# Attention scores as sixteen 32x32 products in four PSUM banks, where four 128x128 products on block-diagonal queries stood

## The reference

```python
qm = _split_heads(q @ Wq.T + bq)      # q = layernorm(x); 16 heads of 32
km = _split_heads(k @ Wk.T + bk)      # k = context, 257 rows
vm = _split_heads(v @ Wv.T + bv)
scores = jnp.einsum('bnlh,bnph->bnlp', qm, km) / np.sqrt(HEAD_DIM)
scores = jnp.where(mask, scores, MASK_FILL)
attn = jax.nn.softmax(scores, axis=-1)
out = jnp.einsum('bnlp,bnph->bnlh', attn, vm)
```

## Time and profile before

| | |
|---|---|
| runs | 1419.02, 1418.9, 1415.56 us, median 1418.9 |
| profiled execution | 1421.52 us, span 1419.4 us |
| busy in the span | PE 1324.6 us (93%), PEld 1020.0 (72%), DVE 774.0 (55%), ACT 632.2 (45%), POOL 392.0 (28%) |
| TensorE instructions | 7110 matmuls, 7111 weight loads |
| granted TensorE clock | 0.981 of full on average |

### The profile page before, as it was taken

The page is one execution under the profiler, slowest core; times in us unless marked ns, Lnnn a source line. Parts: engine busy times, 40 slices in busy tenths (PEclk is TensorE's granted clock), DMA queues, the critical chain, the costliest instruction groups (busy, mean ns, idle before and its releaser), DMA issues. The chain is left out here.

```text
span 1419.4 us, 27453 instructions
## 1 busy us (share of the span) xinstructions
PE 1324.6 (93%) x7110; PEld 1020.0 (72%) x7111; DVE 774.0 (55%) x1808; ACT 632.2 (45%) x1320; POOL 392.0 (28%) x314
## 2 busy tenths in 40 slices
PE   5999999999999999999997888999999999999991
PEld 4888878888888878788886544676677676677670
DVE  4445565565655655655655354665655566655540
ACT  3443344353343433443532114466666566656650
POOL 0001020030030210200300303455555555756441
PEclk9999999999999999999999988999999999999996
DMA  5721110201111101101002105799999999999985
GB/s 199 281 98 32 31 48 17 62 16 39 38 32 31 46 16 31 47 16 54 24 1 71 56 23 208 220 324 324 339 297 303 267 339 306 358 289 314 265 219 87
DMA packets 67184, 204.71 MB, mean 144 GB/s; under 512 B 16047, under 2 KB 18351, under 8 KB 56768
## 3 DMA queue, kind: packets, MB, share of 16 engines
q1 hardware_dynamic: 43248, 159.71, 31.3%
q0 software_dynamic: 23888, 44.40, 14.9%
HBM read 177.26 MB, written 37.03 MB: 151 GB/s over the span
## 5 line engine op out<-in xcount | busy, mean ns | idle before, releaser
L370 POOL TENSOR_TENSOR rstd<-vep,half 128x1 f32<-128x1 f32 x32 | 17.8, 555 | 600.4 <-DVE vep L537 600.3
L856 PE MATMUL bank<-ch,wkh 128*128 128x256 f32 x512 | 160.6, 314 | 8.1 <-DVE cl L548 8.0
L458 ACT ACTIVATE kt<-bank,colb 128x256 f32<-128x256 f32 x128 | 60.5, 472 | 239.1 <-PE bank L858 238.8
L1494 PE MATMUL ebank<-guh,xth 128*128 128x512 f32 x380 | 154.7, 407 | 1.6 <-DVE xtl L1387 1.0
L1382 DVE TENSOR_TENSOR gul<-wgu,guh 128x2048 fp32r<-128x2048 f32 x54 | 123.8, 2293 | 55.3 <-ACT guh L1299 48.4
L1496 PE MATMUL ebank<-guh,xtl 128*128 128x512 f32 x380 | 149.0, 392 | 0.0
L1495 PE MATMUL ebank<-gul,xth 128*128 128x512 f32 x380 | 148.3, 390 | 0.0
L1229 POOL DMA_INDIRECT xg<-xn_rows,ig x95 | 121.3, 1277 | 85.1 <-issue 71.2
L858 PE MATMUL bank<-ch,wkl 128*128 128x256 f32 x512 | 144.3, 282 | 0.0
L857 PE MATMUL bank<-cl,wkh 128*128 128x256 f32 x512 | 144.2, 282 | 0.0
L1524 PE MATMUL ebank<-wd,ht 128*128 128x512 f32 x292 | 134.4, 593 | 0.8 <-ACT ht L1284 0.8
(11 more groups left out here) (247 smaller groups left out, 2817.2 us busy)
## 6 DMA issues: line engine op xcount, KB each, us to landing
wgu<-in_egu SPq DMA_DIRECT2D x54, 1024.0 KB
wd<-in_edn SPq DMA_DIRECT2D x54, 512.0 KB
sgu<-in_egu SPq DMA_DIRECT2D x17, 1024.0 KB
craw<-in_ctx SPq DMA_DIRECT2D x32, 514.0 KB, 3.2
sdn<-in_edn SPq DMA_DIRECT2D x17, 512.0 KB
wqkv<-in_wqkv SPq DMA_DIRECT2D x1, 3072.0 KB, 18.4
second_sums<-x1b SPq DMA_DIRECT2D x9, 256.0 KB, 3.7
xa<-in_x SPq DMA_DIRECT2D x8, 256.0 KB, 2.7
```

Source lines behind the costliest of these rows:

```text
L856: mm(out, wkh[:, c, w], h[:, c, :], start=c == 0, stop=False)
L1494: mm(out, ah[:, c, :], bh[:, c, :], start=c == 0, stop=False)
```

## The change

The scores of a batch become 16 products of a 32x32 weight (the queries of a head, read where the projection left them in `qt`) with 32x257 keys. Product (i, g) uses rows 32i to 32i+31 of the array and its columns 32g to 32g+31, and writes partitions 32g to 32g+31 of bank `sc_ps[i]`. Four banks are used; two of them have other users: bank 0 is also that of the keys and values, and AV moves from bank 5 into the bank of the transposes, bank 4. All 16 stand in slot k = 5, after T1, which is moved there too; AV follows them. `qb`, its zeroing and ACT's four copies a batch go away. As `qt` is now read directly by all four batches, the query projection of the next tile moves from s = 20 of one pass to s = 1 of the next.

```diff
-PRE = {4: "norm", 18: "xT", 20: "q"}
+PRE = {4: "norm", 18: "xT"}
+PREQ = 1
-        kv_ps, sc_ps, at_ps, av_ps, px = bank[0:2], bank[2:4], bank[4], bank[5], bank[6:8]
+        kv_ps, sc_ps, at_ps, av_ps, px = bank[0:2], (bank[2], bank[3], bank[5], bank[0]), bank[4], bank[4], bank[6:8]
...
+                    if front and prev and s == PREQ:
+                        on_pre("q", t)
...
-            def q_blocks(t, b):
-                n = BT * t + b
-                wait(act, s_pqe, t + 1)
-                wait(act, s_sc, 4 * n - 4)
-                for i in range(HG):
-                    r = slice(i * HD, (i + 1) * HD)
-                    last = nc.scalar.copy(qb[b % 2][r, :, i * HD:(i + 1) * HD], qt[r, :, b * L:(b + 1) * L])
-                last.then_inc(s_qb, 1)
...
+                if k == 5 and front:
+                    wait(dve, s_tr, 2 * (n - 1))
+                    wait(dve, s_sc, n + 1)
+                    for i in (HG - 1, *range(HG - 1)):
+                        V.tensor_tensor(prob[b % 2][:, i, :], sc_ps[i][:, 0:S], cap[b % 2][:, :], ALU.min).then_inc(s_sa, 1)
                 if k == 5 and carried:
                     attended(t, b)
-                if k >= 4 and front:
-                    for g in (2 * (k - 4), 2 * (k - 4) + 1):
-
-                        wait(dve, s_sc, 4 * n + g + 1)
-                        if g == 0:
-                            wait(dve, s_tr, 2 * (n - 1))
-                        V.tensor_tensor(prob[b % 2][:, g, :], sc_ps[g % 2][:, 0:S], cap[b % 2][:, :], ALU.min).then_inc(s_sa, 1)
...
+                    if k == 0:
+                        wait(pe, s_sa, 4 * n - 3)
...
+                if k == 5 and carried and front:
+                    prob_t(n, b, 1)
+                if k == 5 and front:
+                    wait(pe, s_ke, 4 * n + 4)
+                    wait(pe, s_ve, 2 * n + 1)
+                    wait(pe, s_sa, 4 * n)
+                    wait(pe, s_pqe, t + 1)
+                    wait(pe, s_pte, t + 2 if b == 3 and nxt else t + 1)
+                    pe.sem_inc(tick, 1)
+                    for g in range(DC):
+                        for i in range(HG):
+                            r = slice(i * HD, (i + 1) * HD)
+                            last = mm(sc_ps[i][g * L:(g + 1) * L, 0:S], qt[r, g, b * L:(b + 1) * L], kt[r, g, :], start=True, stop=True)
+                    last.then_inc(s_sc, 1)
...
-                if k >= 4 and front:
-                    if k == 4:
-                        wait(pe, s_qb, n + 1)
-                    for g in (2 * (k - 4), 2 * (k - 4) + 1):
-                        wait(pe, s_ke, 4 * n + g + 1)
-                        wait(pe, s_sa, 4 * n + g - 1)
...
-                        mm(sc_ps[g % 2][:, 0:S], qb[b % 2][:, g, :], kt[:, g, :], start=True, stop=True).then_inc(s_sc, 1)
-                if k == 4 and carried and front:
-                    prob_t(n, b, 1)
```

More of the change, by code:

```diff
@@ L133, in stage_a @@
         vlc = sb("vlc", [P, DC, NB])
-        qb = [sb(f"qb{i}", [P, DC, P]) for i in range(2)]
+        rows = [sb(f"rows{i}", [P, D]) for i in range(2)]
         prob = d.prob
@@ L163, in stage_a @@
         idx, entry = d.idx, d.entry
-        flat = [a[:, :, :].rearrange("p c s -> p (c s)") for a in (craw[0], craw[1], qb[0], qt, qb[1], xat)]
+        flat = [a[:, :, :].rearrange("p c s -> p (c s)") for a in (craw[0], craw[1], qt, xat)]
+        flat = flat[0:2] + [rows[0][:, :], flat[2], rows[1][:, :], flat[3]]
         sx, sy = [a[:, 0:D] for a in flat[:4]], [a[:, D:2 * D] for a in flat[:2]] + flat[4:]
@@ L168, in stage_a @@
         sht = [wq[:, 3, j * I:(j + 1) * I].rearrange("p (c n) -> p c n", c=IC) for j in range(2)]
-        sd_ps = [at_ps, av_ps]
+        sd_ps = [bank[4], bank[5]]
         s_sl = [sem(f"shared_rows_in{j}") for j in range(SHA)]
@@ L185, in stage_a @@
         s_kv, s_ke, s_ve = sem("kv_projected"), sem("keys_copied"), sem("values_copied")
-        s_qb, s_sc, s_sa = sem("q_blocks"), sem("scores_done"), sem("scores_copied")
+        s_sc, s_sa = sem("scores_done"), sem("scores_copied")
         s_nb, s_ex, s_pn = sem("max_done"), sem("exp_done"), sem("prob_scaled")
@@ L288, in on_pre @@
             def on_pre(n, t):
-                if n == "q":
+                if n == "xT":
                     wait(sp, s_pt, t + 1, tick)
@@ L339, in _ @@
                 load_shared(j, sx[j], sy[j], s_sl[j])
-            sp.wait_ge(s_sc, 4 * NB)
+            sp.wait_ge(s_sc, NB)
             sp.wait_ge(s_pq, NT)
@@ L362, in _ @@
             nc.gpsimd.memset(pad[:, :, 1], 0.0).then_inc(s_pad, 1)
-            for i in range(2):
-                nc.gpsimd.memset(qb[i][:, :, :], 0.0).then_inc(s_pad, 1)
-            pool.wait_ge(s_pad, 4)
+            pool.wait_ge(s_pad, 2)
             def root(n):
@@ L441, in _ @@
             high(0, 0)
-            act.wait_ge(s_pad, 4)
             def exps(b, n, gs):
@@ L456, in per_batch @@
                     wait(act, s_kv, 6 * n + k + 1)
-                    wait(act, s_sc, 4 * n)
+                    wait(act, s_sc, n)
                     nc.scalar.activation(kt[:, k, 0:S1], kv_ps[k % 2][:, 0:S1], ACT.Identity, bias=colb[:, 1, k:k + 1]).then_inc(s_ke, 1)
@@ L461, in per_batch @@
                 if k == 3 and front:
[L462 to L465, removed]
                     if b < 3 or nxt:
@@ L470, in per_batch, with attention @@
                 if k == 4 and carried:
-                    for j in range(2):
-                        wait(act, s_tr, 2 * (n - 1) + j + 1)
-                        nc.scalar.copy(att[:, j, :], at_ps[:, :]).then_inc(s_at, 1)
+                    attention(n, 0)
+                    if not front:
+                        attention(n, 1)
+                if k == 5 and carried and front:
+                    attention(n, 1)
                 if k == 5 and front:
                     values(n, b, k)
-                if k == 5 and front and b == 3 and nxt:
-                    q_blocks(t + 1, 0)
+            def attention(n, j):
+                wait(act, s_tr, 2 * (n - 1) + j + 1)
+                nc.scalar.copy(att[:, j, :], at_ps[:, :]).then_inc(s_at, 1)
             def values(n, b, k):
@@ L655, in on_pre @@
                 if n == "q":
-                    wait(dve, s_qb, 4 * t)
                     pre_q(t)
@@ L877, in per_batch @@
                     wait(pe, s_pn, n)
+                    wait(pe, s_od, n - 1)
                     prob_t(n, b, 0)
@@ L883, in per_batch @@
                     wait(pe, s_ve, 2 * n)
-                    wait(pe, s_od, n - 1)
                     pb = (b - 1) % 2
@@ L887, in per_batch @@
                         w = slice(g * P, (g + 1) * P)
-                        mm(av_ps[:, w], vb[pb][:, 0, w], att[:, 0, w], start=True, stop=False)
-                        last = mm(av_ps[:, w], vb[pb][:, 1, w], att[:, 1, w], start=False, stop=True)
+                        for j in range(2):
+                            heads = att[:, j, :].rearrange("p (i g n) -> p g i n", i=HG, g=DC)[:, g]
+                            last = mm(av_ps[:, w], vb[pb][:, j, w], heads, start=j == 0, stop=j == 1)
                     last.then_inc(s_av, 1)
-                if k >= 4 and front:
-                    if k == 4:
-                        wait(pe, s_qb, n + 1)
-                    for g in (2 * (k - 4), 2 * (k - 4) + 1):
-                        wait(pe, s_ke, 4 * n + g + 1)
-                        wait(pe, s_sa, 4 * n + g - 1)
[L897 to L900, removed]
-                        mm(sc_ps[g % 2][:, 0:S], qb[b % 2][:, g, :], kt[:, g, :], start=True, stop=True).then_inc(s_sc, 1)
-                if k == 4 and carried and front:
-                    prob_t(n, b, 1)
                 if k == 5 and b == 0 and type(t) is int and t == 0:
@@ L912, in on_pre @@
                 if n == "q":
+                    wait(pe, s_sa, 4 * BT * t)
                     pre_q(t)
```

## The result

The changed kernel takes 1489.7 us (median of 4 runs, 1488.97 to 1497.11), the kernel before 1417.7 beside it: a ratio of 1.052, 95% interval 1.049 to 1.055. My 1509 us was in the right direction and inside its range, but that is luck: the 72 us did not come from where I had put them. The sixteen products are far cheaper than the four were, and nearly all of the loss lies in stage B, which the change does not touch.

The account below looks back on a forecast made before the run. PE's list order was taken to bound stage A (busy 739.57 of 762 us). Terms +73 + 27 - 7 - 4 + 1 = +90 us on the median of 1418.9 gave 1509 us, range 1408 to 1522.

Parts of the forecast that it names:

- Only two neighbours overlap: Stage A scores: one product per 0.218 us; with drains 4.03 us a batch against 1.74, +73 us; chance 0.45.
- third rival: Stage A scores: all squares overlap, rows and columns; 1426 us, or 1405 down to 1397 us; chance 0.26.
- The two drains: Array runs empty going from whole-array to small-square matmuls and back, twice a batch: 0.33 us, within the +73 us.
- The change lies wholly in stage A; stage B comes after it and I leave it as it is: Scope of the forecast: only stage A, 14 to 776 us, was given terms; stage B got none.
- The query projection: Moved out of its old place, it leaves T0 waiting for DVE's scaling: 4.5 us in passes 1 to 6, +27 us.
- echo: After T0's wait PE runs some 3 us at 1.2 GHz; T0 to x3T takes 1.38 us more.
- Oproj: Its wait for `ot` falls from 1.3 us to 0.3 or less, 7 times: -7 us.
- T1: Its wait for ACT's copy, 0.14 us in most batches, is covered by half of the values: -4 us.
- oT: Transposes at s = 18 hang on DVE work that now has all four mins ahead of it: +1 us.
- Costed at nothing: ACT's four copies (1.20 us a batch), the first key projection's wait for bank 0, and the later maximum and `nbias`: zero.
- The wait for bank 0: First key projection waits for DVE's reading of scores, covered by AV; without that cover 0.4 us a batch, 13 us.

Follow-up runs that it names:

- the kernel with one row of squares: Changed kernel with 80 extra semaphore increments, all sixteen products reading partitions 0 to 31, so four squares instead of sixteen; measured 1620.5 us.
- the query projection back: Changed kernel with the query projection back at s = 20, a second tile for its result and 74 extra semaphore increments; measured 1410.8 us, ratio 0.995.
- 64 increments: Changed kernel with 64 extra semaphore increments ahead of ACT's loops; measured 1415.5 us, again with ten runs 1418.1 us, ratio 1.0007 to the kernel before.
- 80 increments: Changed kernel with 80 extra semaphore increments at the start of ACT's list; measured 1441.4 us, ratio 1.016 to the kernel before.
- 128 or 208: Changed kernel with 128 or 208 extra semaphore increments ahead of ACT's loops; measured 1499.3 us and 1418.2 us, one run each.
- 58 against 74: Changed kernel with the query projection back at s = 20 and 58 or 74 extra semaphore increments; measured 1403.6 us and 1410.8 us.

## Why the prediction came out as it did

The number was near (1509 for 1489.7, forecast +90, measured +72 beside the same kernel), and for the wrong reason. Two steps failed, by about 104 us one way and 72 the other; that they nearly cancel is luck.

- **"Only two neighbours overlap"**, +73 us, is the step that failed first. From my premise (the second record of a product can't start before the first is through: true, 0.24 us) I went on to "if PE starts its matmuls in the order of the list", and that is not what it does: the next fifteen products' first records start ahead of the second of the first. Starts were to be 0.11 us apart and are 0.0067. The burst takes 0.745 us up to AV. Together with the longer handover from T1 (0.20 for 0.11 us) a batch costs 0.84 us for 1.74. Over stage A the time from start to start falls from 60.1 to 23.8 us for the scores, and rises by 2.9 for the handovers from T1 and by 2.5 for AV: -31 us. That is my third rival, which had 0.26. The Trainium skill's rule in "TensorE: Matmul & The Clock Gate", Part 3, that matmuls stay in program order, was what I leaned on; the starts above do not agree with it for the two records of one fp32 product. Its packing of sixteen squares agrees in kind: it gives the span as one matmul and about 4 ns for each further tile, and here the second record starts 0.24 us behind the first, is 0.375 us long, and the further squares add 15 x 6.7 ns, which makes 0.72 us to the end of the last record.
- **The two drains**, 0.33 us a batch, were about right in size. On the way in, T1's last record holds PE 0.20 us for 0.11. On the way back the changed kernel can't show it: AV starts 0.40 us after the last score record does, but then it is ACT's copy that it waits for. In the kernel with one row of squares, where that copy is long done, AV starts 0.305 us after the last score record, in batches at the full clock, where scores follow each other at 0.217. Its first record then holds PE 0.21 us for 0.11, in both kernels. That is 0.09, 0.09 and 0.10 us, 0.28 in all.
- **"The change lies wholly in stage A; stage B comes after it and I leave it as it is"** failed by 72 us, the whole of the result. The page had the place to ask from: queue 14 fetches instructions, and the change plainly takes instructions out of ACT's list ahead of stage B. Nothing in the profile of before says that a shift of 80 would do harm. It could have been told as a rival with an unknown price; by experiment a bad place costs 72 us in one kernel and 77 in the other.
- **The query projection**, +27 us by 4.5 us a pass. The wait is right: 3.1 us in each of passes 1 to 6. Its echo was under-sized. From the earlier trace rows I took 1.38 us, the part of T0 to x3T alone. In passes 1 to 6 the half clock lasts until the values are well under way, so the starts sum to 26.4 us more for the values, 2.7 for x3T and 5.7 for the router: 35 us, 5.8 a pass. With the query projection back the wait is gone.
- **Oproj**, -7: 5.4 us less wait; the row holds only 6.9 us in six waits, so seven times one was too much. **T1**, -4: the wait for ACT went from 2.0 to 0.7 us, and what handover shrank with it was eaten by the 0.09 us above. **oT**, +1: its start behind xT moves from 0.37 to 0.53 us, 1.0 us in all.
- **Costed at nothing**: the four ACT copies rightly, in time; that they are instructions of code was the whole loss. The wait for bank 0 rightly here. But the cover that I named for it, AV, is not what hides it: it is that VectorE is free, and with the projection back it cost 2.7 us a pass, not the 0.4 us a batch that I gave for a lost cover.

Added up for stage A: -31 for scores and what stands around them, +35, -5, and +1 for oT make 0. With stage B mended by 64 increments, that is what is measured: a ratio of 1.0007.

What stays open: the late stretch of about 5 us once a pass in stage A, which comes with 80 increments and not with 0, 64, 128 or 208. ACT, SyncE and in one kernel PE all slow down in it, at the time of GpSimd's scatters and of the context load, and no instruction fetch is on record there. That it hangs on the number of increments is shown by 64 against 80 (and by 58 against 74 with the projection back); whether it is the place of the code or the time that they take, and what the stretch is, is not. It does not go by the place alone: 208 has the place of 80 against the blocks and not the stretch, and the kernel with one row of squares has 80 increments and no such wait, and its timing differs. No run was made without the scatters.

## What to carry to other kernels

An edit that adds or takes away instructions ahead of a loop can cost more far behind it than it saves where it stands: before explaining a loss by the edit, look at whether the part that got slower was touched at all, at the waits without a releaser, and at the packets of the instruction queue, and shift the code by some tens of empty instructions in both kernels. Small products that each have a square of the array of their own are the thing to build; keep few records to a square in a row. And when work is moved, ask what it was covering where it stood, and which engine's late piece comes into the gap.

## What of the hardware was not expected

- Sixteen fp32 products of 32 rows, 32 columns and 257 moving columns take 0.745 us from the first start to the next matmul of the whole array, 2.3 times faster than four products with whole weights (1.74 us). By my estimate 0.1 us of it is the wait for ACT's copy: the last start at 0.34 us and the 0.305 us to AV of the one-row kernel make 0.65.
- Records of one square follow each other every 0.217 us; with eight of them to a square, the list behind is held up, and the same number of records takes 4.5 us.
- 48 empty instructions on ACT made a kernel 5.4% slower, and 128 on another changed nothing: in stage B the effect is the same again after 128 instructions, or 8192 bytes, in both pairs that were tried (0 and 128, 80 and 208).
- A stop of 3 us of PE was followed by some 7 us at a granted clock near 0.50, which is 1.2 of 2.4 GHz (the windows above), and cost 5.8 us of a pass all in all.
